# Attention scores as two 64-row tiles side by side, two row blocks at a time

## The chip, the cores and the metric

The kernel runs on one core of one Trainium2 chip. The metric is the time of one execution on the device in microseconds, lower is better. Before the change its median over three runs is 1491.43 us (1491.01 to 1491.73).

## What is computed

Sixteen images of 512 channels and 32 by 32 pixels pass a grouped convolution network and then a non-local attention block. Cut to what matters here:

```python
theta = einsum('oc,bcn->bno', theta_w, xf) + theta_b      # 128 channels, 1024 pixels
phi   = einsum('oc,bcn->bon', phi_w, xf) + phi_b[:, None]
g     = einsum('oc,bcn->bno', g_w, xf) + g_b
attn  = softmax(einsum('bno,bom->bnm', theta, phi), axis=-1)   # 1024 x 1024 per image
y     = einsum('bnm,bmo->bno', attn, g)
z     = einsum('co,bno->bcn', w_w, y) + w_b[None, :, None]
```

After that comes a batch norm with given statistics and the residual. The change concerns the product of theta and phi, the scores.

## The kernel before

Everything is written out by hand, engine by engine, with semaphores. The work is pipelined over images: while TensorE does the attention of image n it also does the convolutions of image n + 1, in the order that `batch(n)` of the TensorE block lists. The loop runs 15 times, the last image's attention stands behind it, with a different order (`scores(LAST, i)` between transposes).

- **Projections** (`project`, L441 to L443): three products for each 128 input channels, since each float32 operand is split into a rounded part (`_hi`, type float32r) and the rest (`_lo`), and hi*hi, hi*lo and lo*hi are added up. Full array, 128 rows and 128 columns.
- **Scores** (`scores`, L457 to L459): `i` is one of 8 blocks of 128 query rows. For each of two halves of 512 keys there are the same three products into one PSUM bank, contracting over all 128 channels. Block i uses banks 0 and 1 if i is even, 2 and 3 if it is odd. The last product of the six adds one to `scored`.
- **Behind them**: VectorE takes the maximum of the 1024 scores (`find_max`, L838), ScalarE the exponential and its sum (`exp_row`, L685, two instructions), VectorE the reciprocal of the sum (L844), GpSimd the scaling (L1042), VectorE a transpose in blocks of 32 (L849, `transpose_row`), and a DMA turns the rest. Since two blocks' banks are there for scores, block i may begin when the exponential of block i - 2 is done (`exp_done`).
- **Convolutions** (`mains`, L400, and `left`, L414): 64 by 64 and 32 by 64 tiles of the array in float32, four or eight side by side. One `mains(n, s)` is 16 products, that is 32 instructions in the trace, since each float32 product is issued as two, and each of the two makes two passes over its 512 columns. `dx` (L427) uses four column tiles of 128 by 32.
- **Helper**: `await_ahead(semaphore, value)` puts a wait in front of the next instruction as an instruction of its own.

In the loop the order of TensorE around the scores is:

```python
project(n, 1, PH); project(n, 1, TH)
scores(n, 0); scores(n, 1); project(n, 1, G)
scores(n, 2); scores(n, 3); mains(n + 1, 0)
scores(n, 4); scores(n, 5); left(n + 1, 0)
scores(n, 6); scores(n, 7); mains(n + 1, 1)
```

VectorE does its work in a written order too: the maxima 0 and 1, two reciprocals, the transpose of g (L853), maximum 2, the transpose of row block 0, reciprocal 2, maximum 3, the transposes of 1 and 2, reciprocal 3, maxima 4 and 5, the transpose of 3, reciprocal 4, maxima 6 and 7. ScalarE does exponentials 0 and 1, the bias of g (L675), exponentials 2 to 5, four relus (L657), exponential 6.

Of the kernel before, what the change touches and what calls it, by code (L numbers as in the profile page):

```python
# [10 lines left out]
P = 128  # L11
# [5 lines left out]
HALF = PIXELS // 2  # L17
# [8 lines left out]
QBLOCKS = PIXELS // P  # L26
# [10 lines left out]
CHUNK = 2 * UNIT  # L37
# [27 lines left out]
TH, PH, G = 0, 1, 2  # L65


def conv_attention(nc, x, w_mains, w_lefts, w2_pairs, proj_t, ww, per_channel, out):
    with ExitStack() as ctx:
        def sb(name, shape, dt=F32):  # L70
            return ctx.enter_context(nc.sbuf_tensor(name, shape, dt))

        def sem(name):
            return ctx.enter_context(nc.semaphore(name))
# [16 lines left out]
        tp_hi = sb("tp_hi", [P, 2, PIXELS], F32R)  # L91
        tp_lo = sb("tp_lo", [P, 2, PIXELS], F32R)
# [46 lines left out]
        ps = ctx.enter_context(nc.psum_tensor("ps", [P, 8, HALF], F32))  # L139
# [36 lines left out]
        def split_step(half, w):  # L176
            return SPLIT_PROJECTIONS.index((half, w))
# [27 lines left out]
        hidden_ready = sem("hidden_ready")  # L205
# [4 lines left out]
        projected = sem("projected")  # L210
        proj_biased = sem("proj_biased")
        tp_split = sem("tp_split")
        scored = sem("scored")
        max_found = sem("max_found")
        exp_done = sem("exp_done")
        inv_done = sem("inv_done")
# [20 lines left out]
        LAST = BATCH - 1  # L237
        SLOT_PAIRS = SLOTS * GROUP_PAIRS
# [108 lines left out]
        def _(pe):  # L347
            mm = nc.tensor.matmul
# [71 lines left out]
            def dx(n, s):  # L420
                pe.wait_ge(hidden_ready, n * SLOT_PAIRS + (s + 1) * GROUP_PAIRS)
                if s >= 2:
                    pe.wait_ge(x1_ready, n * SLOTS + s - 1)
                elif not first_image(n):
                    pe.wait_ge(hidden_ready, n * SLOT_PAIRS + 2 * GROUP_PAIRS)
                for q in range(GROUP_PAIRS):
                    last = mm(ps[32 * q:32 * q + 32, dx_bank(s), :], w2s[:, s % GROUPS * GROUP_PAIRS + q, :],  # L427
                              hidden[:, s % HIDDEN_HELD, q, :], start=True, stop=True)
                last.then_inc(dx_summed, 1)

            def project(n, half, w):
                if (half, w) == (0, TH):
                    pe.wait_ge(x1_split, n * SLOTS + GROUPS)
                elif (half, w) == (0, G):
                    pe.wait_ge(tp_split, n * 4 + split_step(0, TH) + 1)
                elif (half, w) == (1, PH):
                    pe.wait_ge(x1_split, n * SLOTS + SLOTS)
                    pe.wait_ge(tp_split, n * 4 + split_step(0, PH) + 1)
                bank = proj_bank(half, w)
                for k in range(BLOCKS):  # L440
                    mm(bank, wp_hi[:, w, k, :], x1_hi[:, half, k, :], start=(k == 0), stop=False)  # L441
                    mm(bank, wp_hi[:, w, k, :], x1_lo[:, half, k, :], start=False, stop=False)  # L442
                    last = mm(bank, wp_lo[:, w, k, :], x1_hi[:, half, k, :], start=False, stop=(k == BLOCKS - 1))  # L443
                last.then_inc(projected, 1)

            def scores(n, i):
                if i == 0:
                    pe.wait_ge(hidden_ready, (n + 1) * SLOT_PAIRS)
                    pe.wait_ge(tp_split, n * 4 + split_step(1, PH) + 1)
                elif i == QBLOCKS // 2:  # L450
                    pe.wait_ge(tp_split, n * 4 + split_step(1, TH) + 1)
                if i >= 2:
                    pe.wait_ge(exp_done, n * QBLOCKS + i - 1)
                rows = slice(i * P, (i + 1) * P)
                for half in range(2):
                    bank, cols = ps[:, 2 * (i % 2) + half, :], slice(half * HALF, (half + 1) * HALF)
                    mm(bank, tp_hi[:, TH, rows], tp_hi[:, PH, cols], start=True, stop=False)  # L457
                    mm(bank, tp_hi[:, TH, rows], tp_lo[:, PH, cols], start=False, stop=False)  # L458
                    last = mm(bank, tp_lo[:, TH, rows], tp_hi[:, PH, cols], start=False, stop=True)  # L459
                last.then_inc(scored, 1)  # L460

            def attend(n, h):
                if h == 0:
# [29 lines left out]
            def batch(n):  # L493
                project(n, 0, TH)
                dx(n, 6)
                dx(n, 7)
                project(n, 0, PH)
                project(n, 0, G)
                project(n, 1, PH)
                project(n, 1, TH)  # L500
                scores(n, 0)
                scores(n, 1)
                project(n, 1, G)
                scores(n, 2)
                scores(n, 3)
                mains(n + 1, 0)
                scores(n, 4)
                scores(n, 5)
                left(n + 1, 0)
                scores(n, 6)  # L510
                scores(n, 7)
                mains(n + 1, 1)
                left(n + 1, 1)
                mains(n + 1, 2)
                left(n + 1, 2)
                dx(n + 1, 0)
                dx(n + 1, 1)
                mains(n + 1, 3)
                left(n + 1, 3)
                attend(n, 0)  # L520
                mains(n + 1, 4)
                output(n, 0, 0)
                output(n, 0, 1)
                left(n + 1, 4)
                output(n, 0, 2)
                output(n, 0, 3)
                mains(n + 1, 5)
                left(n + 1, 5)
                dx(n + 1, 2)
                dx(n + 1, 3)  # L530
                mains(n + 1, 6)
                attend(n, 1)
                left(n + 1, 6)
                output(n, 1, 0)
                output(n, 1, 1)
                dx(n + 1, 4)
                dx(n + 1, 5)
                output(n, 1, 2)
                output(n, 1, 3)
                mains(n + 1, 7)  # L540
                left(n + 1, 7)

                pe.wait_ge(out_added, n * SLOTS + SLOTS)
# [76 lines left out]
            project(LAST, 0, G)  # L620
            project(LAST, 1, PH)
            project(LAST, 1, TH)
            scores(LAST, 0)
            scores(LAST, 1)
            project(LAST, 1, G)
            scores(LAST, 2)
            turn_row(0)
            turn_g()
            scores(LAST, 3)
            turn_row(1)  # L630
            scores(LAST, 4)
            scores(LAST, 5)
            turn_row(2)
            attend_turned(0)
            turn_row(3)
            scores(LAST, 6)
            turn_row(4)
            scores(LAST, 7)
            turn_row(5)
            attend_turned(1)  # L640
            turn_row(6)
# [170 lines left out]
        def _(dve):  # L812
# [21 lines left out]
                    in1=tp_hi[:, w, cols].bitcast(F32), op0=ALU.add, op1=ALU.subtract).then_inc(tp_split, 1)  # L834

            def find_max(n, i):
                dve.wait_ge(scored, n * QBLOCKS + i + 1)
                nc.vector.tensor_reduce(neg_max[:, i % 2:i % 2 + 1], score_banks[i % 2], op=ALU.max, axis=AX.XY,  # L838
                                        negate=True).then_inc(max_found, 1)

# [264 lines left out]
```

## Time and profile before

| | |
|---|---|
| median of 3 runs | 1491.43 us |
| the profiled execution | 1491.56 us, its span 1489.8 us |
| PE (TensorE) busy | 1466.9 us, 98% of the span |
| DVE (VectorE) busy | 832.0 us, 56% |
| ACT (ScalarE) busy | 749.4 us, 50% |
| granted TensorE clock | 9 tenths or more of full speed in every slice of the page, 1.00 over the whole |
| one turn of the image loop | 91.15 us, from one `mains` (L400) at 186.39 us to the same one at 277.54 us |

The page divides the span by engine, by line and by the chain of work that ended last. A PE instruction's duration in the trace overlaps with the next one's, so the pace of a stream of products is read from the distance of starts, not from durations. Times within the program are us from the start of the span.

### The profile page before, as it was taken

The numbers are of one execution on the slowest core, as the hardware profiler recorded it, in microseconds if no ns is written. First come the engines' busy times: TensorE is split into PE (matmuls) and PEld (weight loads), VectorE is DVE, ScalarE is ACT, GpSimd is POOL, SyncE is SP. The second block draws the span as 40 slices with busy tenths as digits, with TensorE's granted clock in tenths as the row PEclk, the third lists the DMA queues.
The fourth block names the chain that finished last, engine by engine and source line by source line (L and its number), as shares of the span: only waits on it lengthen the run. The fifth ranks groups of instructions, "written<-read, shape, count | busy, mean of one in ns | idle before, by whom it ended". The sixth has DMA issues, their size and how long they took to land.

```text
span 1489.8 us, 27659 instructions
## 1 busy us (share of the span) xinstructions
PE 1466.9 (98%) x10364; PEld 772.7 (52%) x10364; DVE 832.0 (56%) x1033; ACT 749.4 (50%) x1175; POOL 241.8 (16%) x134
## 2 busy tenths in 40 slices
PE   7999999999999999999999999999999999999998
PEld 1454636446464464644546455463644636446467
DVE  1374654746546564565646547465474654656456
ACT  3464463645545454455544646446363554645444
POOL 0040210403103030130401204021040210303003
PEclk9999999999999999999999999999999999999999
DMA  4153452535425263261633625346253452535301
GB/s 134 48 185 117 167 202 90 197 113 173 170 90 208 102 209 135 104 232 67 214 127 128 225 81 196 113 160 211 90 196 114 164 179 90 199 110 200 144 29 57
DMA packets 129280, 214.84 MB, mean 144 GB/s; under 512 B 7280, under 2 KB 78448, under 8 KB 129264
## 3 DMA queue, kind: packets, MB, share of 16 engines
q1 hardware_dynamic: 129264, 214.62, 41.4%
q8 instruction: 12, 0.20, 0.1%
q14 instruction: 4, 0.03, 0.0%
HBM read 110.25 MB, written 104.33 MB: 144 GB/s over the span
## 4 chain that ended last, share of the span: by engine, by line
PE 87%; DVE 4%; issue 3%; DMA 3%; ACT 2%; SPq 0%; ACTq 0%
PE ps L400 27%; PE ps L427 8%; PE ps L414 8%; PE ps L441 6%; PE ps L442 6%; PE ps L443 6%; PE ps L471 4%; PE ps L473 4%; PE ps L472 4%; DMA rows_out<-probs 3%; PE ps L487 3%; DVE neg_max L838 2%; PE ps L457 2%; PE ps L459 2%; PE ps L458 2%
## 5 line engine op out<-in xcount | busy, mean ns | idle before, releaser
L400 PE MATMUL ps<-windows,w_main 64*64 64x512 f32 x4096 | 476.1, 598 | 12.1 <-DMA w_left<-in_w_lefts 9.3
L657 ACT ACTIVATE hidden<-ps,columns 128x512 f32<-128x512 f32 x512 | 310.1, 690 | 265.9 <-PE ps L414 265.9
L1042 POOL TENSOR_TENSOR probs<-probs,row_inv 128x1024 f32<-128x1024 f32 x128 | 241.1, 1893 | 1231.7 <-DVE row_inv L844 1231.7
L400 PEld LDWEIGHTS ps<-windows,w_main 64*64 64x64 f32 x4096 | 142.1, 132 | 303.3 <-issue 302.3
L858 DVE TENSOR_TENSOR x_lo<-x_lo,x_hi 128x1024 fp32r<-128x1024 f32 x120 | 153.7, 1301 | 108.2 <-ACT x_hi L692 107.1
L685 ACT ACTIVATE probs<-ps,neg_max 128x1024 f32<-128x1024 f32 x128 | 143.9, 1124 | 126.4 <-DVE neg_max L838 123.4
L838 DVE TENSOR_REDUCE neg_max<-ps 128x1 f32<-128x1024 f32 x128 | 155.7, 1217 | 14.3 <-PE ps L459 10.6
L441 PE MATMUL ps<-x_hi,wp_hi 128*128 128x512 f32 x384 | 153.5, 400 | 0.6 <-issue 0.6
L442 PE MATMUL ps<-x_lo,wp_hi 128*128 128x512 f32 x384 | 150.0, 391 | 0.0
L443 PE MATMUL ps<-x_hi,wp_lo 128*128 128x512 f32 x384 | 149.6, 390 | 0.0
L849 DVE STREAM_TRANSPOSE probs<-probs 128x1024 f32<-128x1024 f32 x120 | 144.6, 1224 | 0.0
L414 PE MATMUL ps<-windows,w_left 32*64 32x512 f32 x2048 | 142.6, 613 | 0.0
L875 DVE SCALAR_TENSOR_TENSOR out_half<-ps,shift,x 128x512 f32<-128x512 f32 x120 | 86.1, 750 | 95.5 <-PE ps L491 94.5
L427 PE MATMUL ps<-hidden,w2s 128*32 128x512 f32 x1024 | 123.7, 599 | 0.0
L827 DVE TENSOR_TENSOR x_lo<-x,x_hi 128x512 fp32r<-128x512 f32 x128 | 82.9, 687 | 72.2 <-ACT x_hi L669 72.1
L692 ACT CAST x_hi<-x_lo 128x1024 fp32r<-128x1024 f32 x120 | 122.3, 1066 | 0.0
L868 DVE TENSOR_TENSOR y_lo<-ps,y_hi 128x512 fp32r<-128x512 f32 x30 | 20.8, 692 | 171.3 <-ACT y_hi L703 171.3
L833 DVE SCALAR_TENSOR_TENSOR tp_lo<-ps,columns,tp_hi 128x512 fp32r<-128x512 f32 x64 | 48.0, 749 | 112.7 <-ACT tp_hi L675 112.7
L820 DVE SCALAR_TENSOR_TENSOR x<-ps,columns,windows 128x512 f32<-128x512 f32 x128 | 95.6, 747 | 24.4 <-PE ps L427 21.3
L457 PE MATMUL ps<-tp_hi 128*128 128x512 f32 x256 | 103.5, 404 | 4.4 <-ACT probs L685 4.4
L703 ACT CAST y_hi<-ps 128x512 fp32r<-128x512 f32 x30 | 17.6, 586 | 169.3 <-PE ps L473 169.3
L459 PE MATMUL ps<-tp_hi,tp_lo 128*128 128x512 f32 x256 | 100.1, 391 | 0.0
(78 smaller groups left out, 1511.7 us busy)
## 6 DMA issues: line engine op xcount, KB each, us to landing
rows_out<-probs SPq DMA_DIRECT2D x120, 512.0 KB, 2.8
x_lo<-rows_out SPq DMA_DIRECT2D x120, 512.0 KB, 5.5
out<-out_half SPq DMA_DIRECT2D x30, 1024.0 KB, 4.2
windows<-in_x SPq DMA_DIRECT2D x64, 298.0 KB, 4.1
windows<-in_x SPq DMA_DIRECT2D x64, 264.0 KB, 5.3
rows_out<-g_t SPq DMA_DIRECT2D x15, 512.0 KB, 2.6
g_raw<-rows_out SPq DMA_DIRECT2D x15, 512.0 KB, 7.3
out<-x SPq DMA_DIRECT2D x8, 256.0 KB, 2.1
```

Source lines behind the costliest of these rows:

```text
L400: product = mm(ps[HIDDEN * which:HIDDEN * (which + 1), hidden_bank(n, s, q), :], w_main[rows, p, which, :], shifted(windows[rows, chunk % ...
L414: last = mm(ps[HIDDEN * which:HIDDEN * (which + 1), hidden_bank(n, s, q), :], w_left[rows, grp, which, :], shifted(windows[rows, unit % UN ...
L427: last = mm(ps[32 * q:32 * q + 32, dx_bank(s), :], w2s[:, s % GROUPS * GROUP_PAIRS + q, :], hidden[:, s % HIDDEN_HELD, q, :], start=True, ...
L441: mm(bank, wp_hi[:, w, k, :], x1_hi[:, half, k, :], start=(k == 0), stop=False)
L442: mm(bank, wp_hi[:, w, k, :], x1_lo[:, half, k, :], start=False, stop=False)
L443: last = mm(bank, wp_lo[:, w, k, :], x1_hi[:, half, k, :], start=False, stop=(k == BLOCKS - 1))
L657: activation(hidden[:, s % HIDDEN_HELD, q, :], ps[:, hidden_bank(n, s, q), :], ACT.Relu, bias=b1s[:, column:column + 1]).then_inc(hidden_r ...
L685: activation(probs[:, i % ROWS_HELD, :], score_banks[i % 2], ACT.Exp, bias=neg_max[:, i % 2:i % 2 + 1], accum_out=row_sum[:, e]).then_inc( ...
L838: nc.vector.tensor_reduce(neg_max[:, i % 2:i % 2 + 1], score_banks[i % 2], op=ALU.max, axis=AX.XY, negate=True).then_inc(max_found, 1)
L849: nc.vector.transpose(row, row).then_inc(transposed, 1)
L858: nc.vector.tensor_tensor(raw, raw.bitcast(F32), pt_hi_squares(i).bitcast(F32), ALU.subtract).then_inc(pt_split, 1)
L1042: nc.gpsimd.tensor_tensor(rows, rows, row_inv[:, e].to_broadcast([P, PIXELS]), ALU.mult).then_inc(normalized, 1)
```

## The change

Each product over 128 channels becomes two over 64 channels: the upper tile works with rows 0 to 63 of the array, the lower one with rows 64 to 127, both over all 128 columns. In the first step the upper tile adds channels 0 to 63 into the bank of the first key half and the lower tile channels 64 to 127 into the bank of the second half; in the second step they change places. Two row blocks (i, i + 1) are done at a time: the first step of i, the first step of i + 1, the second of i, the second of i + 1. Before the second step of a block, TensorE waits until the first step of both tiles has ended (`upper_begun`, `lower_begun`). VectorE waits for two semaphores in place of one. For the last image each block is done alone.

```diff
-            def scores(n, i):
-                if i == 0:
-                    pe.wait_ge(hidden_ready, (n + 1) * SLOT_PAIRS)
-                    pe.wait_ge(tp_split, n * 4 + split_step(1, PH) + 1)
-                elif i == QBLOCKS // 2:
-                    pe.wait_ge(tp_split, n * 4 + split_step(1, TH) + 1)
-                if i >= 2:
-                    pe.wait_ge(exp_done, n * QBLOCKS + i - 1)
-                rows = slice(i * P, (i + 1) * P)
-                for half in range(2):
-                    bank, cols = ps[:, 2 * (i % 2) + half, :], slice(half * HALF, (half + 1) * HALF)
-                    mm(bank, tp_hi[:, TH, rows], tp_hi[:, PH, cols], start=True, stop=False)
-                    mm(bank, tp_hi[:, TH, rows], tp_lo[:, PH, cols], start=False, stop=False)
-                    last = mm(bank, tp_lo[:, TH, rows], tp_hi[:, PH, cols], start=False, stop=True)
-                last.then_inc(scored, 1)
+            def scores(n, rows):
+                for i in rows:
+                    if i == 0:
+                        await_ahead(hidden_ready, (n + 1) * SLOT_PAIRS)
+                        await_ahead(tp_split, n * 4 + split_step(1, PH) + 1)
+                    elif i == QBLOCKS // 2:
+                        await_ahead(tp_split, n * 4 + split_step(1, TH) + 1)
+                for step in range(2):
+                    for i in rows:
+                        if step == 0 and i >= 2:
+                            await_ahead(exp_done, n * QBLOCKS + i - 1)
+                        elif step == 1:
+                            await_ahead(upper_begun, n * QBLOCKS + i + 1)
+                            await_ahead(lower_begun, n * QBLOCKS + i + 1)
+                        queries = slice(i * P, (i + 1) * P)
+                        for m, (one, two) in enumerate([(tp_hi, tp_hi), (tp_hi, tp_lo), (tp_lo, tp_hi)]):
+                            for tile in range(2):
+                                rows64 = slice(CHUNK * tile, CHUNK * (tile + 1))
+                                half = (tile + step) % 2
+                                keys = slice(half * HALF, (half + 1) * HALF)
+                                product = mm(ps[:, 2 * (i % 2) + half, :], one[rows64, TH, queries],
+                                             two[rows64, PH, keys], start=(step == 0 and m == 0),
+                                             stop=(step == 1 and m == 2), skip_group_check=True)
+                                if m == 2 and step == 0:
+                                    product.then_inc(upper_begun if tile == 0 else lower_begun, 1)
+                                elif m == 2:
+                                    product.then_inc(scored_upper if tile == 0 else scored_lower, 1)
...
-                scores(n, 0)
-                scores(n, 1)
+                scores(n, (0, 1))
                 project(n, 1, G)
-                scores(n, 2)
-                scores(n, 3)
+                scores(n, (2, 3))
                 mains(n + 1, 0)
-                scores(n, 4)
-                scores(n, 5)
+                scores(n, (4, 5))
                 left(n + 1, 0)
-                scores(n, 6)
-                scores(n, 7)
+                scores(n, (6, 7))
...
-            scores(LAST, 3)
+            scores(LAST, (3,))
...
             def find_max(n, i):
-                dve.wait_ge(scored, n * QBLOCKS + i + 1)
+                dve.wait_ge(scored_upper, n * QBLOCKS + i + 1)
+                dve.wait_ge(scored_lower, n * QBLOCKS + i + 1)
```

How TensorE's instructions stand for row blocks 6 and 7 in the loop (`out<-in`, the shape, what the instruction waits for). Before, behind the eight `left` products, block 6 is six products, and block 7's begin with the wait for its exponential:

```order
L414 MATMUL ps<-windows,w_left 64x512 x8
L457 MATMUL ps<-tp_hi 128x512 [waits exp_done]
L458 MATMUL ps<-tp_lo,tp_hi 128x512
L459 MATMUL ps<-tp_hi,tp_lo 128x512
L457 MATMUL ps<-tp_hi 128x512
L458 MATMUL ps<-tp_lo,tp_hi 128x512
L459 MATMUL ps<-tp_hi,tp_lo 128x512
L457 MATMUL ps<-tp_hi 128x512 [waits exp_done]
```

After the change the four parts of the pair 6 and 7 stand like this, six products in each part:

```order
L417 MATMUL ps<-windows,w_left 64x512 x8
L471 MATMUL ps<-tp_hi 128x512 [waits exp_done]
L471 MATMUL ps<-tp_hi 128x512
L471 MATMUL ps<-tp_lo,tp_hi 128x512 x2
L471 MATMUL ps<-tp_hi,tp_lo 128x512 x2
L471 MATMUL ps<-tp_hi 128x512 [waits exp_done]
L471 MATMUL ps<-tp_hi 128x512
L471 MATMUL ps<-tp_lo,tp_hi 128x512 x2
L471 MATMUL ps<-tp_hi,tp_lo 128x512 x2
L471 MATMUL ps<-tp_hi 128x512 [waits upper_begun,lower_begun]
```

The second wait for an exponential, that of block 7, now stands ahead of the second step of block 6, and so ahead of everything that completes block 6.

For the last image, where a block is alone, the second step comes right behind the first:

```order
L471 MATMUL ps<-tp_hi 128x512 [waits hidden_ready,tp_split]
L471 MATMUL ps<-tp_hi 128x512
L471 MATMUL ps<-tp_lo,tp_hi 128x512 x2
L471 MATMUL ps<-tp_hi,tp_lo 128x512 x2
L471 MATMUL ps<-tp_hi 128x512 [waits upper_begun,lower_begun]
L471 MATMUL ps<-tp_hi 128x512
```

Nothing stands between the third pair of products and the wait for its end.

## Rows read from the trace of the kernel before

**Rows 1.** The page: busy time, share of the span, instructions.

```profile
PE 1466.9 (98%) x10364; PEld 772.7 (52%) x10364; DVE 832.0 (56%) x1033; ACT 749.4 (50%) x1175; POOL 241.8 (16%) x134
```

**Rows 2.** Waits of PE from 70 to 1430 us: total us, times, longest.

```profile
PE ps L457 <- ACT probs L685: 3.6, 15, 0.2
```

**Rows 3.** Timeline of PE, one image: start, duration, what.

```profile
166.97 0.39 PE L443 MATMUL ps<-x_hi,wp_lo 128*128 128x512 f32 x1
167.20 0.39 PE L457 MATMUL ps<-tp_hi 128*128 128x512 f32 x1
...
169.69 0.39 PE L459 MATMUL ps<-tp_hi,tp_lo 128*128 128x512 f32 x1
...
172.41 0.39 PE L443 MATMUL ps<-x_hi,wp_lo 128*128 128x512 f32 x1
...
175.13 0.39 PE L459 MATMUL ps<-tp_hi,tp_lo 128*128 128x512 f32 x1
175.45 3.66 PE L400 MATMUL ps<-windows,w_main 64*64 64x512 f32 x32
179.04 0.50 PE L457 MATMUL ps<-tp_hi 128*128 128x512 f32 x1
179.38 0.39 PE L458 MATMUL ps<-tp_lo,tp_hi 128*128 128x512 f32 x1
...
180.31 0.39 PE L459 MATMUL ps<-tp_hi,tp_lo 128*128 128x512 f32 x1
...
183.34 0.50 PE L457 MATMUL ps<-tp_hi 128*128 128x512 f32 x1 [0.24 <-ACT probs L685]
...
186.32 3.67 PE L400 MATMUL ps<-windows,w_main 64*64 64x512 f32 x32
189.92 1.11 PE L414 MATMUL ps<-windows,w_left 32*64 32x512 f32 x16
190.96 3.67 PE L400 MATMUL ps<-windows,w_main 64*64 64x512 f32 x32
```

**Rows 4.** Timeline of the weight loads (PEld), same image.

```profile
175.93 0.15 PEld L400 LDWEIGHTS ps<-windows,w_main 64*64 64x64 f32 x4 [0.28 <-issue]
...
178.08 0.15 PEld L400 LDWEIGHTS ps<-windows,w_main 64*64 64x64 f32 x4 [0.28 <-issue]
...
179.38 0.19 PEld L459 LDWEIGHTS ps<-tp_hi,tp_lo 128*128 128x128 f32 x1
```

**Rows 5.** Timeline of DVE, same image.

```profile
168.79 2.55 DVE L838 TENSOR_REDUCE neg_max<-ps 128x1 f32<-128x1024 f32 x2
...
173.56 1.25 DVE L853 STREAM_TRANSPOSE g_t<-g_t 128x1024 f32<-128x1024 f32 x1 [0.78 <-ACT g_t L675]
174.73 1.19 DVE L838 TENSOR_REDUCE neg_max<-ps 128x1 f32<-128x1024 f32 x1
...
177.28 1.23 DVE L838 TENSOR_REDUCE neg_max<-ps 128x1 f32<-128x1024 f32 x1
...
180.75 2.57 DVE L838 TENSOR_REDUCE neg_max<-ps 128x1 f32<-128x1024 f32 x2
```

**Rows 6.** Timeline of ACT, same image.

```profile
171.38 1.12 ACT L685 ACTIVATE probs<-ps,neg_max 128x1024 f32<-128x1024 f32 x1
172.39 0.19 ACT L685 ACTIVATION_READ_ACCUMULATOR probs<-ps,neg_max 128x1 f32 x1
172.84 0.69 ACT L675 ACTIVATE g_t<-ps,columns 128x512 f32<-128x512 f32 x1 [0.26 <-PE ps L443]
...
178.54 1.11 ACT L685 ACTIVATE probs<-ps,neg_max 128x1024 f32<-128x1024 f32 x1 [1.39 <-DVE neg_max L838]
179.55 0.19 ACT L685 ACTIVATION_READ_ACCUMULATOR probs<-ps,neg_max 128x1 f32 x1
...
182.08 1.11 ACT L685 ACTIVATE probs<-ps,neg_max 128x1024 f32<-128x1024 f32 x1 [2.34 <-DVE neg_max L838]
183.09 0.19 ACT L685 ACTIVATION_READ_ACCUMULATOR probs<-ps,neg_max 128x1 f32 x1
```

More of the change, by code:

```diff
@@ L212, in conv_attention @@
         tp_split = sem("tp_split")
-        scored = sem("scored")
+        upper_begun = sem("upper_begun")
+        lower_begun = sem("lower_begun")
+        scored_upper = sem("scored_upper")
+        scored_lower = sem("scored_lower")
         max_found = sem("max_found")
@@ L622, in _ @@
             project(LAST, 1, TH)
-            scores(LAST, 0)
-            scores(LAST, 1)
+            scores(LAST, (0,))
+            scores(LAST, (1,))
             project(LAST, 1, G)
-            scores(LAST, 2)
+            scores(LAST, (2,))
             turn_row(0)
             turn_g()
-            scores(LAST, 3)
+            scores(LAST, (3,))
             turn_row(1)
-            scores(LAST, 4)
-            scores(LAST, 5)
+            scores(LAST, (4,))
+            scores(LAST, (5,))
             turn_row(2)
@@ L635, in _ @@
             turn_row(3)
-            scores(LAST, 6)
+            scores(LAST, (6,))
             turn_row(4)
-            scores(LAST, 7)
+            scores(LAST, (7,))
             turn_row(5)
```

## The prediction

> **What bounds the kernel now.** I read the page first: TensorE is busy for 98% of the span [rows 1], so what matters is its order of work, what each product takes and where it waits. Next the waits of TensorE: in the loop it waits in one place, 15 times, once an image, for an exponential, 0.24 us each [rows 2, 3]. So everything that TensorE does longer, or waits longer, is paid in full, unless it falls into these 3.6 us. Then the timelines of one image, of TensorE, its weight loads, VectorE and ScalarE [rows 3 to 6]. The reader is to see that around row blocks 0 to 7 the three engines hand work round: scores, maximum, exponential, and back to TensorE, which needs the bank. That circle has hardly any slack: exponential 3 ends at 179.55 + 0.19 = 179.74 [rows 6] and block 5 begins six products after 179.04, near 180.5; exponential 4 ends at 183.28 [rows 6] and block 6 begins at 183.34 [rows 3].
>
> **The change, part by part.** All times are those of this one image; what comes after it repeats.
>
> *1. The products.* Before: 11 steps from 167.20 to 169.69 [rows 3], 0.2264 us for each full-array product. Six make a block, 1.36 us. After, twelve half-products of 64 rows make six pairs. No row shows a float32r product in tiles of 64 by 128. The nearest by shape are the 64 by 64 tiles of `mains`: four loads begin together at 175.93 and again up to 178.08, five turns of two passes [rows 4], 0.43 us a turn or 0.215 a pass; there four tiles run side by side. The nearest by type is the full-array product itself, 0.2264. I take 0.215 for a pair (the tiles run side by side, and the shape is what changes), a gain of 0.0114 x 6 = 0.07 us a block, 0.55 an image. The bounds are 0.2264 (no gain) and 0.240 (two weight loads of 128 columns to a pair, of which each exposes a little; the excess over 0.2264 is as large as the gain).
>
> The trace shows weight loads hidden in the full-array form too: a load of 0.19 us begins at 179.38 [rows 4], together with the product before it [rows 3], and the pace stays near 0.23 us. The Trainium skill ("TensorE: Matmul & The Clock Gate", What overlaps and what doesn't) says that a weight load overlaps a running product only where the row group differs. By that rule the old form would show its load in each product and alternating row tiles would hide it; 0.11 x 6 x 128 = 84 us would be won. This trace does not agree, and the sum goes by the rows.
>
> *2. Changes of the array's form.* From full array to tiles: the last L459 starts at 175.13, L400 at 175.45 [rows 3]: 0.32, of which 0.23 is the product, so 0.09 is lost. The first load of a stretch is not covered: the first L457 after tiles takes 0.50 where others take 0.39 [rows 3], so 0.11 for 128 columns. From tiles back: 179.04 - 175.45 = 3.59 against 8 turns of 0.43, and some 0.05 of the 0.15 over is the first load of 64 columns: 0.10 lost. So an entry into score tiles costs 0.20 and an exit 0.21. Scores that lay among projections without a change now have an entry (blocks 0 and 1), an exit (projection G) and an entry (2 and 3): 0.61 us more an image. The changes at `mains` and `left` were there before. Bounds: each 0.02 to 0.15 for the loss apart from the load. On TensorE alone parts 1 and 2 come out at 0.61 - 0.55, nothing.
>
> *3. The order of two blocks.* This is the large part. A block used to be done six products after its start. Now the first of a pair is done after nine pairs and the second after twelve, since the first step of the second stands between; and the second block's bank is wanted three pairs after the start in place of six products. Both ends of the circle shrink by about 0.65 us. I walk it.
>
> - Blocks 0 and 1 enter at 166.97 + 0.23 + 0.09 = 167.29, the first pair goes at 167.40. Block 0's last pair starts 8 x 0.215 later, 169.12, and ends 0.39 later, 169.51. With two semaphores I let its maximum follow by 0.08, since ScalarE's exponential with one wait follows its maximum by 0.03 (177.28 + 1.23 to 178.54) and block 4's, with two, by about 0.1 (182.08 after the maximum begun at 180.75) [rows 5, 6]. So maximum 0 begins at 169.59, and two of 1.23 end at 172.05 (before: 168.79 + 2.55 = 171.34 [rows 5]).
> - Exponential 1 begins 0.03 later and takes 1.20 with its sum, to 173.28 (before: 172.39 + 0.19 = 172.58). The bias of g waited for it already, with 0.26 between [rows 6], and comes at 173.54. The transpose of g follows 0.72 behind, at 174.26, where it was 173.56 [rows 5]: +0.70. VectorE keeps its order, so maximum 2, transpose 0, maximum 3 and exponential 3 all come 0.70 later, and exponential 3 ends at 180.44. The scores are no later than that: projection G ends its starts at 172.69, blocks 2 and 3 enter at 173.01, block 2 is done at 175.23, maximum 2 begins at 174.73 + 0.70 = 175.43.
> - Blocks 4 and 5 enter at 179.38 (0.34 later than before). Block 5's first step would go at 179.49 + 0.645 = 180.14; it waits for exponential 3 until 180.50 (TensorE follows ScalarE by 0.06: 183.28 to 183.34), and then shows its first load, 180.61. In TensorE's queue the second step of block 4 stands behind that wait, and VectorE waits for it. Its last pair starts 0.645 + 2 x 0.215 later and block 4 is done at 182.08; before, at 180.31 + 0.39 = 180.70 [rows 3]. Maximum 4 begins at 182.16, not 180.75, exponential 4 at 183.49, not 182.08, and it ends at 184.69.
> - Blocks 6 and 7 enter at 184.75 (before: 183.34), since `left` is over at 183.7. Maximum 5 and exponential 5 run behind 4's; exponential 5 ends at 186.04. Block 7's first step, due at 185.51, goes at 186.21. The last pair starts 0.645 + 5 x 0.215 later, 187.93, and `mains` 1 begins at 188.23, where it was 186.32 [rows 3]: **+1.91 us an image**.
>
> Behind that the relus, exponentials 6 and 7 and the split of the turned rows come up to 2.6 us later. `mains` 2 needs exponential 7 for its second couple 0.9 us after 190.96 + 1.91 [rows 3], about 193.8, and I get 192.6 for its end. What else there is follows TensorE and moves along. Nothing returns the 1.91. 15 images: 28.7 us. With 0.2264 for a pair the walk gives 2.2, with form changes of 0.15 and 0.2264 it gives 2.4, with 0.240 2.6; with form changes of 0.02 and 0.215 it gives 1.8. If waiting in the queue does not expose the loads, 0.2 less, 1.6.
>
> *4. The last image.* Each block alone waits for the end of its first step: 0.39 + 0.05 + 0.11 for the load in place of 0.215, +0.34, less 0.07 for the pace, +0.27. Blocks 0 to 2 with two entries and two exits come to 0.81 + 0.7 = 1.5 us; the other five come to 1.35 + four entries and exits of 0.3, 2.6, of which I count half, because there TensorE waits for exponentials and splits anyway. 2.8 us; bounds 1.5 and 4.1.
>
> **Sum.** 1491.56 + 28.7 + 2.8 = 1523.1 us. The profiled execution lies 0.13 us over the median, so 1523 for the median.
>
> **The rivals.**
>
> *Slower, as walked*: 1512 to 1536. For it: TensorE has no slack [rows 1], and the circle is tight at blocks 5 and 6. 0.74.
>
> *Slower by less*, 1497 to 1511: the delay of exponentials 0 to 3 is absorbed, and only the wait of block 7 for exponential 5 remains, some 0.7 us an image, 15 x 0.7 + 2.8 = 13 us. Against it: the rows show VectorE going from one wait to the next with 0.04 us between. 0.09.
>
> *No change*: the walk is wrong throughout and parts 1 and 2 cancel, 0.06 us an image. 0.06.
>
> *Faster*: pairs at 0.215, 128 x 0.07 = 9 us won, form changes between score tiles and full array that cost nothing (both use all 128 columns), and no wait that grows: 1483. It decides from the point where exponential i - 2 is over three pairs after a pair's start. By the rows, with nothing moved, exponential 3 ends at 179.74, and block 5 would want it at 179.04 + 0.11 + 0.65 = 179.80: only just, and block 7 not, since exponential 5 could not end before 184.5 and is wanted at 184.1. 0.07.
>
> *The tiles don't run side by side*: each half-product takes its 0.215 alone, 128 x 6 x 0.215 = 165 us more, 1690 in all. The 64 by 64 and 32 by 64 tiles overlap in the trace (32 instructions of `mains` in 3.6 us [rows 3], each of two passes), so there is no reason for it but the type. 0.04.
>
> **How the numbers follow.** The first two and the last are slower: 0.87. The likeliest is 1523. The walk's own bounds give 15 x 1.6 + 1.5 = 25.5 us, 1517, and 15 x 2.6 + 4.1 = 43.1 us, 1535. The range goes to 1508 at the low end, to take in part of the second case, and to 1536. What lies outside is 0.04 at 1690, 0.13 for no change or faster, and a few in a hundred between 1497 and 1508. Differences under 0.2%, 3 us, can hardly be told from none with this kernel.
>
> **What the profile will show.** Pairs of L471 0.215 apart, two products within 0.01 us of each other (wrong if 0.43 apart). Maximum 0 later by 0.8 us from its pair's start, block 5's first step held for exponential 3 and block 7's for exponential 5, some 0.4 and 0.7 us; waits of TensorE for exponentials of 1 to 2 us an image in all, where there were 0.24. A turn of the loop of 93.1 us in place of 91.15. It is wrong if TensorE's waits stay at 0.24 us, if the turn is under 92 us, or if a pair takes over 0.25.

## The result and the profile after

The change makes the kernel slower: 1535.28 us median (1534.98 to 1536.01, 4 runs) against 1491.58 us (1491.01 to 1491.84, 4 runs), a ratio of 1.0294 with a 95% interval of 1.0276 to 1.0312. The profiled execution took 1536.01 us, its span 1534.0 us. The forecast was 1523, in a range of 1508 to 1536: the direction was right, and the time lies in the range, 0.7 us below its upper end. The forecast added 31.5 us; the measured time adds 43.7.

The page of the changed kernel, its busy row; then TensorE's waits in the loop (70 to 1440 us):

```profile
PE 1491.8 (97%) x11132; PEld 777.6 (51%) x11132; DVE 843.4 (55%) x1033; ACT 747.5 (49%) x1175; POOL 241.8 (16%) x134
```

```profile
PE ps L471 <- ACT probs L698: 20.7, 30, 1.1
```

Against [rows 1] TensorE is 24.9 us longer at work, with 768 half-products more, and against [rows 2] it waits for exponentials twice an image and 17 us more.

Now one image on TensorE (start, duration, what; two tiles of a pair are merged to "x2"), to be laid beside [rows 3]:

```profile
264.32 0.39 PE L446 MATMUL ps<-x_hi,wp_lo 128*128 128x512 f32 x1
264.64 0.50 PE L471 MATMUL ps<-tp_hi 64*128 64x512 f32 x2
264.97 0.40 PE L471 MATMUL ps<-tp_lo,tp_hi 64*128 64x512 f32 x2
...
267.29 0.39 PE L471 MATMUL ps<-tp_hi,tp_lo 64*128 64x512 f32 x2
267.61 0.50 PE L444 MATMUL ps<-x_hi,wp_hi 128*128 128x512 f32 x1
...
270.25 0.39 PE L446 MATMUL ps<-x_hi,wp_lo 128*128 128x512 f32 x1
270.57 0.50 PE L471 MATMUL ps<-tp_hi 64*128 64x512 f32 x2
...
273.22 0.40 PE L471 MATMUL ps<-tp_hi,tp_lo 64*128 64x512 f32 x2
273.62 3.66 PE L403 MATMUL ps<-windows,w_main 64*64 64x512 f32 x32
277.21 0.50 PE L471 MATMUL ps<-tp_hi 64*128 64x512 f32 x2
...
277.78 0.40 PE L471 MATMUL ps<-tp_hi,tp_lo 64*128 64x512 f32 x2
278.46 0.51 PE L471 MATMUL ps<-tp_hi 64*128 64x512 f32 x2 [0.28 <-ACT probs L698]
...
282.93 0.51 PE L471 MATMUL ps<-tp_hi 64*128 64x512 f32 x2 [1.08 <-ACT probs L698]
...
283.47 0.44 PE L471 MATMUL ps<-tp_hi,tp_lo 64*128 64x512 f32 x2
284.03 0.50 PE L471 MATMUL ps<-tp_hi 64*128 64x512 f32 x2
...
286.29 3.66 PE L403 MATMUL ps<-windows,w_main 64*64 64x512 f32 x32
```

Four things are to be seen. The tiles do run side by side, but a pair is no faster than a full-array product: (267.29 - 264.64 - 0.11)/11 = 0.231 us. The full-array products of projection G that follow take the same, (270.25 - 267.61 - 0.11)/11 = 0.230, and in the kernel before so did blocks 6 and 7, which also stand right behind a change of the array's form:

```profile
183.68 0.39 PE L458 MATMUL ps<-tp_lo,tp_hi 128*128 128x512 f32 x1
...
186.00 0.40 PE L459 MATMUL ps<-tp_hi,tp_lo 128*128 128x512 f32 x1
```

That is (186.00 - 183.68)/10 = 0.232. The 0.2264 of [rows 3] is a stream that has run on for a while. So the pair loses nothing by its form; the first float32r products behind a change of form, up to about a dozen, lose some 0.005 each, whatever the form. Each change of form costs 0.32 - 0.23 = 0.09 and a bare load, 0.50 in place of 0.39. Block 5's first step follows block 4's by 0.68 in place of 0.23 (277.78 to 278.46), block 7's follows 6's by 0.56. And block 6 waits 1.08 us for exponential 4, where it was 0.24.

The cause of that last one is on VectorE and ScalarE:

```profile
279.28 0.12 DVE L858 RECIPROCAL row_inv<-row_sum 128x1 f32<-128x1 f32 x1
280.24 2.36 DVE L852 TENSOR_REDUCE neg_max<-ps 128x1 f32<-128x1024 f32 x2 [0.84 <-PE ps L471]
```

```profile
278.13 0.19 ACT L698 ACTIVATION_READ_ACCUMULATOR probs<-ps,neg_max 128x1 f32 x1
281.58 1.11 ACT L698 ACTIVATE probs<-ps,neg_max 128x1024 f32<-128x1024 f32 x1 [3.26 <-DVE neg_max L852]
282.60 0.19 ACT L698 ACTIVATION_READ_ACCUMULATOR probs<-ps,neg_max 128x1 f32 x1
282.69 1.11 ACT L698 ACTIVATE probs<-ps,neg_max 128x1024 f32<-128x1024 f32 x1
```

VectorE (the first of the two views) is free at 279.40 and idles 0.84 us until block 4 is done; before, it went on to maximum 4 after 0.04 [rows 5]. So exponential 4 ends at 282.79 and TensorE, whose `left` is long over, starts block 6 at 282.93.

One turn of the loop, from the starts of L403 (L400 before) in the timelines, `mains` 0 to `mains` 1 to the next `mains` 0; the kernels below are the experiments:

| kernel | starts | mains 0 to 1 | rest | turn |
|---|---|---|---|---|
| before | 175.45, 186.32, 266.61 | 10.87 | 80.29 | 91.16 |
| the change | 179.85, 192.54, 273.62 | 12.69 | 81.08 | 93.77 |
| e1 full array, pair order | 176.25, 188.44, 268.72 | 12.19 | 80.28 | 92.47 |
| e2 tiles, single | 183.57, 196.37, 279.83 | 12.80 | 83.46 | 96.26 |
| e3 waits attached | 179.44, 192.02, 273.06 | 12.58 | 81.04 | 93.62 |
| e6 tiles, blocks 4 to 7 | 177.46, 189.92, 270.22 | 12.46 | 80.30 | 92.76 |
| e7 tiles, blocks 0 to 3 | 177.28, 188.51, 269.58 | 11.23 | 81.07 | 92.30 |
| e8 tiles in the last image | 176.68, 187.73, 267.99 | 11.05 | 80.26 | 91.31 |
| e9 one semaphore | 177.91, 190.25, 271.38 | 12.34 | 81.13 | 93.47 |
| e10 before, maximum's wait last | 174.46, 185.24, 265.51 | 10.78 | 80.27 | 91.05 |
| e11 e3 + e9 + e10 | 178.98, 191.21, 272.23 | 12.23 | 81.02 | 93.25 |

The change adds 1.82 us between `mains` 0 and 1 and 0.79 in the rest, which is the stretch ahead of `mains` 0, 15 x 2.61 = 39 us. The last part, from the start of the last `mains` 7 (1422.68 before, 1462.90 after) to the end, is 71.1 us in place of 67.1, 4.0 more. About 0.6 us more lie in the first image's start, where also kernels with the same code there differ: `mains` of the second image starts at 84.33 in the kernel before and at 83.45 in e10.

### The profile page after: what moved, and what is told of

Its sections match the earlier page's. It is cut to its first block, busy times and chain, and to the rows that moved or that the text cites. A ratio compares the mean times of both kernels' runs of the same rounds, so it can differ in the third digit from the quotient of the medians.

```text
span 1534.0 us, 29721 instructions
## 1 busy us (share of the span) xinstructions
PE 1491.8 (97%) x11132; PEld 777.6 (51%) x11132; DVE 843.4 (55%) x1033; ACT 747.5 (49%) x1175; POOL 241.8 (16%) x134
## 4 chain that ended last, share of the span: by engine, by line
PE 90%; issue 4%; DVE 4%; ACT 2%; DMA 0%; SPq 0%; DVEq 0%; ACTq 0%
PE ps L403 27%; PE ps L471 11%; PE ps L430 8%; PE ps L417 8%; PE ps L444 6%; PE ps L445 6%; PE ps L446 6%; PE ps L488 4%; PE ps L490 4%; DVE neg_max L852 4%; PE ps L489 4%; PE ps L504 3%; PE ps L505 2%; PE ps L508 2%; ACT probs L698 1%
## 5 line engine op out<-in xcount | busy, mean ns | idle before, releaser
L403 PE MATMUL ps<-windows,w_main 64*64 64x512 f32 x4096 | 476.7, 599 | 12.2 <-DMA w_left<-in_w_lefts 9.3
L403 PEld LDWEIGHTS ps<-windows,w_main 64*64 64x64 f32 x4096 | 144.7, 132 | 302.2 <-issue 302.2
L872 DVE TENSOR_TENSOR x_lo<-x_lo,x_hi 128x1024 fp32r<-128x1024 f32 x120 | 163.8, 1385 | 91.5 <-ACT x_hi L705 91.5
L852 DVE TENSOR_REDUCE neg_max<-ps 128x1 f32<-128x1024 f32 x128 | 152.5, 1221 | 67.1 <-PE ps L471 64.8
L471 PE MATMUL ps<-tp_hi 64*128 64x512 f32 x512 | 113.7, 430 | 25.2 <-ACT probs L698 20.7
L882 DVE TENSOR_TENSOR y_lo<-ps,y_hi 128x512 fp32r<-128x512 f32 x30 | 20.7, 692 | 171.2 <-ACT y_hi L716 171.2
L471 PE MATMUL ps<-tp_hi,tp_lo 64*128 64x512 f32 x512 | 104.3, 390 | 0.0
L471 PE MATMUL ps<-tp_lo,tp_hi 64*128 64x512 f32 x512 | 103.7, 388 | 0.0
```

The lines of the kernel that those rows point to most:

```text
L403: product = mm(ps[HIDDEN * which:HIDDEN * (which + 1), hidden_bank(n, s, q), :], w_main[rows, p, which, :], shifted(windows[rows, chunk % ...
L471: product = mm(ps[:, 2 * (i % 2) + half, :], one[rows64, TH, queries], two[rows64, PH, keys], start=(step == 0 and m == 0), stop=(step == ...
L872: nc.vector.tensor_tensor(raw, raw.bitcast(F32), pt_hi_squares(i).bitcast(F32), ALU.subtract).then_inc(pt_split, 1)
```

## The experiments

**e1: the order alone.** Full-array products and single waits as before, two blocks at a time in the new order.

```diff
+                for half in range(2):
+                    for i in rows:
+                        if half == 0 and i >= 2:
+                            pe.wait_ge(exp_done, n * QBLOCKS + i - 1)
...
+                        mm(bank, tp_hi[:, TH, queries], tp_hi[:, PH, cols], start=True, stop=False)
...
-                scores(n, 4)
-                scores(n, 5)
+                scores(n, (4, 5))
```

> Full-array products as before, but two row blocks at a time in the new order (first key half of i, first key half of i + 1, second of i, second of i + 1); no tiles, no change of form, no wait for own products; the last image as before. My theory (the order prolongs the circle of scores, maximum and exponential): the walk with a pace of 0.2267 and no entries gives +1.7 us from mains 0 to mains 1 of an image, nothing ahead of mains 0, so 15 x 1.7 = 26 us, about 1517. Rival (form changes, the slower pair and the separate waits are what costs): within 3 us of 1491.6.

Measured: 1511.74 us, ratio 1.0134 (1.0117 to 1.0150). The turn is 1.31 us longer, all of it between `mains` 0 and 1. The timeline shows the same picture as the change:

```profile
273.26 0.50 PE L459 MATMUL ps<-tp_hi 128*128 128x512 f32 x1
...
275.53 1.11 PE L414 MATMUL ps<-windows,w_left 32*64 32x512 f32 x16
277.56 0.50 PE L459 MATMUL ps<-tp_hi 128*128 128x512 f32 x1 [0.92 <-ACT probs L684]
...
278.13 0.39 PE L461 MATMUL ps<-tp_hi,tp_lo 128*128 128x512 f32 x1
278.66 0.50 PE L459 MATMUL ps<-tp_hi 128*128 128x512 f32 x1
```

So 20 of the 43.7 us need no tile at all: they are the price of finishing two blocks together. The rival that only forms, pace and waits cost is out. The walk had 1.7; it was 0.4 too long.

**e2: tiles, one block at a time.** `scores(n, (0, 1))` and so on become `scores(n, (0,))`, `scores(n, (1,))`.

> The tiles of the change, one row block at a time in the loop too, so that the second step waits for the end of the first with nothing between. The circle is shorter than with pairs of blocks, but each block has a hole: 0.39 + 0.05 + 0.11 in place of 0.23, 0.34 us, or 0.43 if a separate wait costs 0.09 more; 8 blocks 2.7 to 3.4 us an image, of which a part covers waits. If the order of two blocks is all that costs, this is faster than the change: 1510 to 1520. If the hole is paid in full, the walk gives +3.3 us an image, 49 us, and 4 for the last image: about 1544.

Measured: 1572.78 us, ratio 1.0543 (1.0526 to 1.0561), beyond both expectations. TensorE waits for no exponential any more, but for itself:

```profile
PE ps L471 <- PE ps L471: 30.7, 108, 0.3
```

```profile
289.12 0.39 PE L471 MATMUL ps<-tp_hi,tp_lo 64*128 64x512 f32 x2
289.81 0.50 PE L471 MATMUL ps<-tp_hi 64*128 64x512 f32 x2 [0.30 <-PE ps L471]
290.12 0.43 PE L471 MATMUL ps<-tp_lo,tp_hi 64*128 64x512 f32 x2
```

From the third pair to the fourth 0.69, to the fifth 0.31, where both would be 0.23: the hole costs 0.54 us, not 0.34 to 0.43. Eight of them are 4.3 us of the 5.10 that the turn is longer, and the tiles' forms the rest. Of the holes only the 0.24 us are covered that TensorE waited for exponential 4 before: between `mains` 0 and 1 four of them are 2.16, and that part is 1.93 longer. So the pair order is the cheaper of the two ways to give the tiles their places, and still dear.

**e3: waits attached to the instruction.** All `await_ahead` in the scores become `pe.wait_ge`.

> The change with its waits attached to the next instruction, as the score waits were before, not as instructions of their own. In the trace of the change TensorE follows an exponential by about 0.14 to 0.2 us where it was 0.06, at two places an image, and mains 0 starts 0.08 late behind a row of such waits. If these cost what they seem to, 0.2 to 0.3 us an image are won, 3 to 5 us: 1530 to 1532. If TensorE's queue hid them, no difference.

Measured: 1532.72 us, ratio 1.0272 (1.0255 to 1.0290), 2.6 us less than the change. The turn is 0.15 us shorter. It is a small cost, a little under what was expected. In the loop `mains` 0 follows the last pair by 0.32 us again, as before, not by the change's 0.40:

```profile
272.74 0.39 PE L471 MATMUL ps<-tp_hi,tp_lo 64*128 64x512 f32 x2
273.06 3.67 PE L403 MATMUL ps<-windows,w_main 64*64 64x512 f32 x32
```

In the last image the hole of a block that is alone is smaller, 0.57 + 0.31 less 0.46 = 0.42 us where e2 had 0.54, since TensorE follows the end of its own products by 0.18 and not by 0.30:

```profile
1481.54 0.40 PE L471 MATMUL ps<-tp_hi,tp_lo 64*128 64x512 f32 x2
1482.11 0.50 PE L471 MATMUL ps<-tp_hi 64*128 64x512 f32 x2 [0.18 <-PE ps L471]
```

**e8: tiles in the last image alone.** In the loop full-array products one block at a time, which still add to `scored_upper` after the one key half and to `scored_lower` after the other, so that VectorE keeps its two waits.

```diff
+                    last = mm(bank, tp_lo[:, TH, rows], tp_hi[:, PH, cols], start=False, stop=True)
+                    last.then_inc(scored_upper if half == 0 else scored_lower, 1)
```

> Tiles in the last image alone (each block by itself, as in the change), full array in the loop. The trace of the change shows the last part 4.0 us longer; by my step 4 it was 2.8. Expected: 1494.4 to 1495.6. If the longer last part came from the loop's end instead, no difference.

Measured: 1498.80 us, ratio 1.0045 (1.0028 to 1.0062), more than expected. The last part is what the change has, 1497.2 - 1426.17 = 71.0 us. What I had not expected is the loop: its turn is 0.15 us longer than before though TensorE's products and their order are the same. What differs is the second wait on VectorE and the increments that the products carry (those on `upper_begun` and `lower_begun` among them). e9 was made to tell the two apart.

**e6 and e7: the two halves of the loop.** Tiles in pairs for blocks 4 to 7 alone, and for 0 to 3 alone, the others as in e8, the last image full array.

> In the loop tiles in pairs for row blocks 4 to 7 alone, which lie between convolution tiles anyway; blocks 0 to 3 full array, one at a time; last image full array. No additional change of form. If the order of two blocks is the main cost, it is here: the trace of the change has 1.8 us between mains 0 and mains 1, so 15 x 1.8 = 27 us, about 1518. If the form changes around blocks 0 to 3 are the main cost, 1495 or less.

> The other half: tiles in pairs for blocks 0 to 3 alone, with three additional changes of form, blocks 4 to 7 full array and one at a time; last image full array. The trace of the change has 0.83 us ahead of mains 0; blocks 4 to 7 then follow exponential 3 and 4, which come 0.4 later or so but are wanted later too. Expected 15 x 0.8 to 0.9 = 12 to 14 us, about 1505. With the run for blocks 4 to 7 and the last image alone it should add up to 44 us; more or less says that the halves act on each other.

Measured: e6 1515.84 us, 1.0158 (1.0141 to 1.0175); e7 1508.98 us, 1.0113 (1.0096 to 1.0129). The turn is 1.60 and 1.14 us longer, 0.15 of each for the second semaphore: 1.45 + 0.99 + 0.15 = 2.59, and the change has 2.61. The halves add up. e7 is 4 us above the 1505 expected, because of its 0.36 between `mains` 0 and 1, where I had counted 0.05. Its "rest" is the change's, 81.07 and 81.08: this is the three additional changes of form, with the slower pace behind each.

**e4 and e5: type or shape?** The score operands read as float32, each product then being two instructions of two passes; e4 in the full array, e5 in the tiles. The scores take four times the passes, so only the pace is compared.

```diff
-                    mm(bank, tp_hi[:, TH, rows], tp_hi[:, PH, cols], start=True, stop=False)
+                    mm(bank, tp_hi[:, TH, rows].bitcast(F32), tp_hi[:, PH, cols].bitcast(F32), start=True, stop=False)
```

> Before, with the score operands read as float32 in place of float32r: each product becomes two instructions of two passes, so the scores take four times as long; only the pace is of interest. If the 13 ns over 512 columns that a float32r product takes (0.2267 against 0.2133 us at 2.4 GHz) belong to the full array, an instruction of two passes takes 0.440; if they belong to the type, 0.428 to 0.430 as in the convolution tiles.

> The change with the score operands read as float32. Pairs of 64 by 128 tiles: 0.428 to 0.430 for two passes if the 0.230 of the change come from the type float32r, 0.44 or more if they come from the 128 columns or from a pair's weight loads.

Each ran once, 1967.78 and 2044.20 us. The weight loads, one with each instruction, show the pace, first e4, then e5:

```profile
699.10 0.19 PEld L459 LDWEIGHTS ps<-tp_hi,tp_lo 128*128 128x128 f32 x1 [0.24 <-issue]
...
703.82 0.19 PEld L458 LDWEIGHTS ps<-tp_lo,tp_hi 128*128 128x128 f32 x1 [0.24 <-issue]
```

```profile
712.09 0.19 PEld L471 LDWEIGHTS ps<-tp_hi 64*128 64x128 f32 x2 [0.24 <-issue]
...
714.24 0.19 PEld L471 LDWEIGHTS ps<-tp_hi,tp_lo 64*128 64x128 f32 x2 [0.24 <-issue]
```

e4: (703.82 - 699.10)/11 = 0.429 for two passes; e5: (714.24 - 712.09)/5 = 0.430. The shape makes no difference, the type does: 0.2145 to 0.215 a pass in float32, 0.2264 in float32r in a long full-array stream, and 0.230 to 0.232 behind a change of form, in the full array as in pairs.

**e9: one semaphore for a block's end.**

```diff
-                                    product.then_inc(scored_upper if tile == 0 else scored_lower, 1)
+                                    product.then_inc(scored_upper, 1)
...
-                dve.wait_ge(scored_upper, n * QBLOCKS + i + 1)
-                dve.wait_ge(scored_lower, n * QBLOCKS + i + 1)
+                dve.wait_ge(scored_upper, 2 * (n * QBLOCKS + i + 1))
```

> The change with one semaphore for the end of a block: both tiles add one to it and VectorE waits for twice the count. The run with tiles in the last image alone has full-array scores in the loop and the change's two semaphores, and its turn is 0.15 us longer than before. If the second wait of each maximum costs that, this kernel wins 15 x 0.15 = 2.3 us over the change and a few tenths in the last image: 1532 to 1533. Rival (the 0.15 is from the increments that TensorE's products carry, not from the wait): no difference, 1535.

Measured: 1529.63 us, ratio 1.0250 (1.0236 to 1.0264), 5.6 us less than the change. The increments stay, the second wait is gone, so it was the wait. The turn is 0.30 shorter, twice what was expected. Maximum 3 shows why, first in the change, then in e9:

```profile
275.56 0.16 DVE L858 RECIPROCAL row_inv<-row_sum 128x1 f32<-128x1 f32 x1
275.85 1.23 DVE L852 TENSOR_REDUCE neg_max<-ps 128x1 f32<-128x1024 f32 x1
```

```profile
273.25 0.17 DVE L857 RECIPROCAL row_inv<-row_sum 128x1 f32<-128x1 f32 x1
273.35 1.23 DVE L851 TENSOR_REDUCE neg_max<-ps 128x1 f32<-128x1024 f32 x1
```

Both blocks had long been scored, and yet the maximum comes 0.29 after the reciprocal's start with two waits and 0.10 with one. e8, with full-array products and two waits, shows the same:

```profile
178.42 0.16 DVE L881 RECIPROCAL row_inv<-row_sum 128x1 f32<-128x1 f32 x1
178.72 1.23 DVE L875 TENSOR_REDUCE neg_max<-ps 128x1 f32<-128x1024 f32 x1
```

Maximum 4, which does wait for its scores, follows the end of block 4's last pair by 0.11 us in the change and by 0.03 in e9. 15 x 0.30 = 4.5 us; the other 1.2 us are in the first image's start (`mains` of the second image), which varies.

**e10: before, the maximum's wait last.**

```diff
-                act.wait_ge(max_found, n * QBLOCKS + i + 1)
                 if i >= ROWS_HELD:
...
                         act.wait_ge(row_sent[i - ROWS_HELD], (n + 1) * 16)
+                act.wait_ge(max_found, n * QBLOCKS + i + 1)
```

> Before, with one thing moved: from block 4 on ScalarE's exponential waits first for the DMA that frees its row and then for the maximum, so that the wait that comes last is the one on the instruction. Before, exponential 3 follows its maximum by 0.03 us and 4 by 0.12, and TensorE waits 0.24 an image for exponential 4. If a wait on the instruction is 0.09 quicker, 15 x 0.09 = 1.4 us are won, 1490.4, 0.1%, at the edge of what can be told; the profile should show TensorE's wait at 0.15. If not, no difference.

Measured: 1490.12 us against 1492.09, ratio 0.9986 (0.9977 to 0.9995). VectorE's maxima 4 and 5, and ScalarE's exponential 4:

```profile
179.76 2.57 DVE L838 TENSOR_REDUCE neg_max<-ps 128x1 f32<-128x1024 f32 x2
```

```profile
181.01 1.11 ACT L685 ACTIVATE probs<-ps,neg_max 128x1024 f32<-128x1024 f32 x1 [2.25 <-DVE neg_max L838]
```

```profile
PE ps L457 <- ACT probs L685: 1.8, 12, 0.2
```

The exponential starts 1.25 after its maximum, before 1.33 [rows 5, 6], TensorE waits half as long as in [rows 2], and the turn is 0.11 shorter. That is 1.6 us in 15 turns. The profiled executions are 2.4 apart, of which 0.88 stand ahead of `mains` of the second image (84.33 and 83.45), where no exponential that the edit touches has run; so some 1.5 us are the edit's. This small step is the only version here that is faster than the kernel before, and so than both.

**e11: the change with lighter waits.** The edits of e3, e9 and e10 in one.

> The change with all three: waits of TensorE attached to the next instruction, one semaphore for a block's end, the maximum's wait last for the exponential. The first alone won 2.6 us. If the three add up: 1535.3 - 2.6 - 2.5 - 1.4 x 2 = 1527 to 1530; what is left over before, 37 us, is then the order, the forms and the last image. If the waits overlap with one another, 1531 to 1532.5.

Measured: 1526.29 us, ratio 1.0230 (1.0216 to 1.0244), 9.0 us less than the change, and a little under the 1527 to 1530 expected. It is what the tiles cost with waits as light as I could make them: 34 us.

## Why the prediction was right, and where its sizes were off

**The mechanism was right, for half of the cost.** Two blocks at a time finish later, and want their banks earlier, than one after the other, and around blocks 4 to 7 there was too little slack for it. e1 shows 1.31 us an image for the order without any tile, half of the 2.61 by which the turn is longer. The other half is 0.8 us for the part ahead of `mains` 0 (e7), 0.30 for the second wait (e9) and 0.15 for the waits as instructions of their own (e3). Together that is 2.6. These were taken one at a time and need not add up so well: they meet in the same waits, and the 0.08 at `mains` 0 is in two of them.

**That the time fell inside the range was in part luck.** The 43.7 us lie just past the walk's own bound of 43.1. An image was forecast at +1.91 and came at +2.61. Of the missing 0.70, 0.45 stand ahead of `mains` 0 (forecast 0.34, 175.79 against 175.45; measured 0.79) and 0.25 behind it. 15 x 0.70 = 10.5 us, with 1.2 of the last image and 0.6 of the first image's start, is the whole miss of 12.2. Against that, the walk counted 1.7 for the order alone where e1 has 1.31; without this error the forecast would have been lower still. Of the signs, the waits came (20.7 us in 15 images, 1.4 each) and a turn over 92 us; the pairs stand 0.231 apart, not 0.215.

**Step 1, the pace, was mis-sized.** I took 0.215 for a pair, from the float32 tiles, a gain of 0.55 us an image. It is 0.231. The neighbour of the same type was in the rows, and I chose by shape where e4 and e5 show that the type decides. What I also missed is that float32r products are slower behind a change of form. The change puts blocks 0 and 1, projection G and blocks 2 and 3 there: from the last product ahead of block 0 to `mains` 0 there are 33 such steps, of 0.231 in place of 0.2264 to 0.2267, 0.14 us. With 0.6 for the three changes of form and 0.08 at `mains` 0 that is the 0.8, and so "TensorE alone comes out at nothing" was wrong. The rule of the Trainium skill ("TensorE: Matmul & The Clock Gate", What overlaps and what doesn't) that a weight load is hidden only behind a product of another row group was rightly left out of the sum: no gain of 84 us came.

**Step 2, the forms, was right**: 0.09 and a bare load of 0.11 at each, as the rows of the change show at 264.64, 267.61 and 270.57. The Trainium skill, "TensorEngine Tiling (Array Packing)", Key Properties, says that a change of the tiling mode drains TensorE; these rows fit that, with 0.09 us beside the load. What I missed is `mains` 0, which starts 0.40 after the last pair, not 0.32. The separate waits are the cause: with them attached (e3) it is 0.32 again. The whole part ahead of `mains` 0 gets 0.04 shorter by it.

**Step 3, the walk, was right in its places, and less so in its path.** Predicted and measured: from `mains` 0 to 1 +1.57 and +1.82; the wait of block 6 behind `left` 1.05 and 1.08; block 5's first step late by 0.47 and 0.54, block 7's by 0.70 and 0.40, each with its bare load. Block 7's is smaller because exponential 5 ended 1.10 us behind exponential 4 (282.79 to 283.89), where I had 1.35.

Three things were wrong in it. The first is the part on the bias of g: it "waited for" exponential 1 "already". It did not; the row says that it waited 0.26 for TensorE (`<-PE ps L443` in [rows 6]). e1 shows that slack: exponential 1 starts 3.62 us ahead of `mains` 0 (268.72), where before it was 4.07 (171.38 and 175.45), so 0.45 later, and the bias of g 2.51 ahead in place of 2.61, only 0.10 later:

```profile
265.10 1.12 ACT L684 ACTIVATE probs<-ps,neg_max 128x1024 f32<-128x1024 f32 x1
266.21 0.68 ACT L674 ACTIVATE g_t<-ps,columns 128x512 f32<-128x512 f32 x1
```

The second is how maximum 2 is held. I had it wait for VectorE's own order, behind the transpose of g, and wrote that the scores are no later than that. In the change it waits 0.41 us for TensorE, and comes 0.98 later than before where I had 0.70 (8.74 us after the product ahead of block 0, before 7.76), since projection G and blocks 2 and 3 lost the pace that I had given them:

```profile
273.06 1.23 DVE L852 TENSOR_REDUCE neg_max<-ps 128x1 f32<-128x1024 f32 x1 [0.41 <-PE ps L471]
```

The third is the second wait on VectorE, for which I took 0.05 more at each maximum. By e9 it costs 0.19 at maximum 3, where the block was long done, and 0.30 us an image. Exponential 3 nevertheless ends 4.70 us after `mains` 0 begins, where I had 4.65: both were later than forecast, by about the same, and that is why the places behind `mains` 0 fit better than what went into them. Had the pace been 0.2264 my walk gave 2.2, its highest variant with 0.240 gave 2.6: the measured 2.61 is at that end.

**Step 4, the last image, was mis-sized**: 2.8 us, measured 4.0, near its upper bound of 4.1. The hole between the steps is 0.54 us and not 0.34 (e2): TensorE follows its own products only 0.30 us after their end (289.12 + 0.39 to 289.81), not 0.05. I had taken the 0.05 from TensorE's reaction to ScalarE, with a single wait attached to the instruction. The separate waits are 0.12 of the difference (e3: 0.18 us after the end, and a last part of 1530.7 - 1460.38 = 70.3 us in place of 71.1). The sum of this step also has 0.7 for two entries and two exits, which by step 2 are 0.82, and 0.3 for each of the later four, without a row.

**The rivals.** *Slower by less* fell: the delay of exponential 1 was in part absorbed, as e1 shows, but the wait behind `left` for exponential 4 was not. *No change* and *faster* rested on the pace of 0.215, which no stream of float32r products in these traces reaches. *Tiles one after the other* fell by 0.231. Two things stay open: why a float32r product takes 0.012 us more than a float32 pass, and why the first products behind a change of form take 0.005 more again. No run here was made for either.

## What to carry to other kernels

Before work is interleaved, walk the circle of producer, reader and free buffer: two items finished together take slack away on both sides, and here a TensorE that is always busy paid for what was lacking. Splitting a product that already fills the array into row tiles gains nothing here, and costs a change of form on each side, an exchange of places to wait for, and more semaphores. Take the pace of a product from a row of the same type and the same place, in a long stream or behind a change of form; its shape mattered less here. And where an instruction waits for two things, use one counter, or place the wait that comes last next to the instruction.

## What the hardware showed that I had not expected

- Two waits in front of a VectorE instruction delay it even if both are long fulfilled: 0.29 and 0.30 us after the start of the instruction before it (the change, e8), in place of 0.10 with one (e9).
- On ScalarE the order of two waits matters: 1.33 us from the maximum's start to the exponential's with the late wait first, 1.25 with it last (before, e10), worth some 1.5 us of 1492.
- At a granted clock of 1.00 a pass over 512 columns takes 0.2145 us in float32, in the full array and in tiles (e4, e5). In float32r it takes 0.2264 in a long full-array stream and 0.230 to 0.232 in the stretches of twelve behind a change of form, in the full array (before, the change) and in pairs of 64-row tiles (the change) alike.
- TensorE waiting for the end of its own products goes on 0.30 us after it with two waits as instructions of their own (e2), and 0.18 with the waits attached to the product (e3).
